# A new order for the first pair of the last stage, with two expansions inside the last convolution, and earlier middle rows behind the half quads

## What is computed

```python
for t in range(3):                                    # first block, on _gn(x)
    attn = softmax(q . (x @ Wk)); pooled = attn . (x @ Wv)
    weights = softmax(masked(pooled @ Wmlp) / 1.5); wsel = top 2 of 4, rescaled
    x_mod = x * (1 + attn_map * S * softplus(alpha))
    x = sum_e wsel[e] * conv3x3(x_mod, We[e], be[e])
x = x0 + x                                            # first residual
n = _gn(x)                                            # group norm, 32 groups
r = relu(batchnorm(n @ Wr + br)); w = r @ Ws + bs     # 9 taps for each of 16 groups
xi = n @ Wi + bi
out = x + sum over 9 taps of w * shifted(xi)          # involution, second residual
```

## Time and profile before

| | |
|---|---|
| median of three runs | 655.09 us (654.85 to 655.28) |
| the profiled execution | 654.83 us, span 653.0 us |
| PE busy | 618.9 us, 95% of the span |
| DVE busy | 529.7 us, 81% |
| ACT busy | 330.7 us, 51% |
| POOL busy | 179.1 us, 27% |
| mean granted clock of PE | 0.988 |
| share of the chain that ended last | PE 68%, DVE 10% |

### The profile page before, as it was taken

The page is one execution under the profiler, slowest core; times in us unless marked ns, Lnnn a source line. Parts: engine busy times, 40 slices in busy tenths (PEclk is TensorE's granted clock), DMA queues, the critical chain, the costliest instruction groups (busy, mean ns, idle before and its releaser), DMA issues.

```text
span 653.0 us, 15558 instructions
## 1 busy us (share of the span) xinstructions
PE 618.9 (95%) x6032; PEld 257.8 (39%) x6032; DVE 529.7 (81%) x836; ACT 330.7 (51%) x455; POOL 179.1 (27%) x193
## 2 busy tenths in 40 slices
PE   6868999989999999999999999989999999999995
PEld 6533333323343433343333434323444444444442
DVE  5789874998667977895798899768888988888885
ACT  3755443422342233233314657745777887787761
POOL 2100250005500640091028003412432342244230
PEclk9989899999999999999999999998999999999998
DMA  9940030024444245325512542000122221312222
GB/s 322 221 82 2 1 79 9 1 52 119 98 100 97 74 98 124 71 74 127 134 39 67 141 117 75 1 9 10 42 51 54 60 49 42 73 41 50 47 68 65
DMA packets 67462, 48.75 MB, mean 75 GB/s; under 512 B 53602, under 2 KB 54596, under 8 KB 67396
## 3 DMA queue, kind: packets, MB, share of 16 engines
q1 hardware_dynamic: 67108, 47.60, 29.8%
q10 hardware_dynamic: 288, 0.21, 0.1%
HBM read 35.94 MB, written 9.76 MB: 70 GB/s over the span
## 4 chain that ended last, share of the span: by engine, by line
PE 68%; DVE 10%; issue 2%; ACT 0%; DVEq 0%; ACTq 0%
PE conv L829 18%; PE conv L887 12%; PE att L903 12%; PE conv L750 10%; PE att L573 4%; PE att L652 2%; PE att L664 2%; PE att L874 2%; PE conv L769 2%; DVE xpad L1391 2%; DVE x L1763 1%; PE conv L780 1%; DVE xpad L1444 1%; DVE x L1456 1%; PE att L631 1%
## 5 line engine op out<-in xcount | busy, mean ns | idle before, releaser
L1763 DVE TENSOR_TENSOR x<-conv,x 128x512 f32<-128x512 f32 x288 | 177.8, 682 | 24.9 <-PE conv L887 23.6
L829 PE MATMUL conv<-xpad,comb 64*64 64x512 f32 x1728 | 194.1, 593 | 0.1
L829 PEld LDWEIGHTS conv<-xpad,comb 64*64 64x64 f32 x1728 | 70.4, 134 | 104.8 <-issue 102.5
L887 PE MATMUL conv<-rstack,wse 98*128 98x512 f32 x288 | 95.2, 433 | 2.7 <-DVE xin L1523 0.9
L903 PE MATMUL att<-x,cmp 64*32 64x512 f32 x1280 | 80.6, 602 | 0.0
L887 PEld LDWEIGHTS conv<-rstack,wse 98*128 98x128 f32 x288 | 48.1, 188 | 72.1 <-DVE x L1763 65.4
L1024 ACT ACTIVATE comb<-experts,small 128x768 f32<-128x768 f32 (+1 forms) x33 | 28.2, 879 | 83.9 <-PE conv L750 37.6
L1391 DVE SCALAR_TENSOR_TENSOR xpad<-att,x 128x1024 f32<-128x1024 f32 x46 | 54.3, 1212 | 18.6 <-PE att L631 18.4
L1915 POOL TENSOR_TENSOR x<-x,xin 128x1024 f32<-128x1024 f32 x15 | 35.9, 2394 | 111.6 <-ACT x L1189 111.6
L1033 ACT ACTIVATE x<-conv,bias 128x512 f32<-128x512 f32 x36 | 22.7, 681 | 75.0 <-PE conv L829 56.1
L750 PE MATMUL conv<-xpad,comb 64*64 64x512 f32 x480 | 56.4, 598 | 4.3 <-DVE x L1456 4.3
(11 more groups left out here) (225 smaller groups left out, 802.1 us busy)
## 6 DMA issues: line engine op xcount, KB each, us to landing
experts<-forms SPq DMA_DIRECT2D x88, 192.0 KB, 4.0
x<-in_x SPq DMA_DIRECT2D x32, 256.0 KB, 5.3
experts<-forms SPq DMA_DIRECT2D x56, 144.0 KB, 2.9
out<-comb SPq DMA_DIRECT2D x30, 256.0 KB, 3.2
rstack<-rstack SPq DMA_DIRECT2D x16, 128.0 KB, 2.3
experts<-in_We SPq DMA_DIRECT2D x1, 1152.0 KB
forms<-experts SPq DMA_DIRECT2D x2, 576.0 KB, 5.7
out<-comb SPq DMA_DIRECT2D x4, 128.0 KB, 2.2
```

Source lines behind the costliest of these rows:

```text
L829: last = nc.tensor.matmul(conv[own[to], h, HW * rows:HW * rows + HW], comb[own[rows], q % 2, n, tap(t)], xpad[own[rows], 2 * (q % 2) + n, ...
L887: nc.tensor.matmul(conv[:, unit, cols], wse[:, ORDER[i], :], rstk[s][0:RR, cols], start=True, stop=True).then_inc(exp_full, 1)
L1763: v.tensor_tensor(img(prod[i])[:, rows, :], img(conv[:, unit, :])[:, rows, :], xip[s][:, kh + 16 * h:kh + 16 * h + 16, kw:kw + W], ALU.mul ...
```

## The change

1. **Behind the half quads.** `hurried` leaves out quads 11 and 15, so ACT makes both of their first scaled weights and DVE's L1507 falls away there. In quads 10 and 14 `ahead` is (0,), so `middle_rows` comes behind one `modulate` instruction instead of two.
2. **Two expansions inside the last convolution.** In half 1 of quad 23, `project_xi` of pair 0 moves from behind tap 2 to behind tap 1; the expansion of index 0 stands behind tap 4 and that of index 2 behind tap 6, both in unit 0. DVE makes their products before `final(23, 1)`.
3. **Order of pair 0.** Expansions and products come in the order 0, 2, 4, 1, 6, 3, 8, 5, 7. An expansion waits for the product of index i - 2. `project` of pair 1 stands ahead of index 4, `project_xi` between 3 and 8, and the three rounds of `add_up` at the end.
4. **Statistics of quad 23** are taken by ACT (`late_stats`, with `fin` as scratch) between `empty_r` and `empty_xi` of pair 1, not by DVE between the products.
5. **Around it.** On DVE the wait for `nmr_ready` 5 stands ahead of `add_residual(22)`, and the instruction that completes `wse` moves behind it. POOL makes scale and shift (`inverse_root(4)`) after the first of two pairs of memsets. ACT waits for the pads ahead of `empty_xi` and no longer ahead of the first normalisation.

```diff
-            return q - 1 in SHORT and q % QP == QP - 1 and q < QP * LAST
+            return q - 1 in SHORT and q % QP == QP - 1 and q < QP * LAST and q - 2 not in HALF
...
-                    elif at == (3, 1, 2):
+                    elif at == (3, 1, 1):
                         project_xi(0, 0, 1)
+                    elif at == (3, 1, 4):
+                        eng.wait_ge(wse_ready, 1)
+                        eng.wait_ge(final_emptied, FINAL_PARTS - 2)
+                        expand(0, 0, AHEAD[0])
+                    elif at == (3, 1, 6):
+                        expand(0, 0, AHEAD[1])
...
+            def involve_first():
+
+                project(1, 1, 2)
+                expand(0, 0, 4)
+                eng.wait_ge(final_emptied, FINAL_PARTS)
+                expand(0, 0, 1)
+                expand(0, 0, 6)
+                expand(0, 0, 3)
+                project_xi(1, 1, 3)
+                expand(0, 0, 8)
+                expand(0, 0, 5)
+                add_up(0, 0)
+                expand(0, 0, 7)
+                add_up(0, 1)
+                add_up(0, 2)
...
                     empty_r(k + 1, 1 - s, m)
+                    if first:
+                        for n in range(2):
+                            late_stats(QUADS - 1, n, GP + QP + n, fin)
                     empty_xi(1 - s, m + 1)
...
-                            ahead = (0,) if j == 0 or q == QUADS - 2 else (0, 1)
+                            ahead = (0,) if j == 0 or q == QUADS - 2 or q - 1 in HALF else (0, 1)
...
-            final(QUADS - 1, 1)
-            eng.wait_ge(final_emptied, FINAL_PARTS)
-
...
             def involve(k, s, first=False):
-                for i in range(TAPS):
+                for i in (FIRST_ORDER[2:] if first else range(TAPS)):
                     product(k, s, i, first)
-                    if first and i in (1, 3):
-                        channel_stats(slot(QUADS - 1, i // 2))
-
+
+            for i in AHEAD[:2]:
+                product(0, 0, i, True)
+            final(QUADS - 1, 1)
+            eng.wait_ge(final_emptied, FINAL_PARTS)
```

More of the change, by code:

```diff
@@ L133, with turn_of, upto_round @@
 PARTS_OF_SUM = 4
+AHEAD = (0, 2)
+FIRST_ORDER = (0, 2, 4, 1, 6, 3, 8, 5, 7)
+def turn_of(k, i):
+    return FIRST_ORDER.index(i) if isinstance(k, int) and k == 0 else k * TAPS + i
+def upto_round(k, r):
+    if isinstance(k, int) and k == 0:
+        return max(FIRST_ORDER.index(i) for i in ROUNDS[r]) + 1
+    return k * TAPS + ROUNDS[r][-1] + 1
 def build(nc, A, out):
@@ L667, in project_xi, with expand @@
                 last.then_inc(misc_full, 1)
+            def expand(k, s, i):
+                e = turn_of(k, i)
+                unit = (s * TAPS + i) % 2
+                if i == 0:
+                    eng.wait_ge(rstk_ready, k + 1)
+                    eng.wait_ge(rhi_copied[s], 8 * (k - s) + 16)
+                for h, cols in halves():
+                    if isinstance(k, int) and k == 0 and i > 1:
+                        eng.wait_ge(prod_ready, 2 * turn_of(k, i - 2) + h + 1)
+                    elif isinstance(k, int) and k == 1 and i == 0:
+                        eng.wait_ge(prod_ready, 2 * turn_of(0, TAPS - 2) + h + 1)
+                    elif not (isinstance(k, int) and k == 0):
+                        eng.wait_ge(prod_ready, 2 * (e - 2) + h + 1)
+                    nc.tensor.matmul(conv[:, unit, cols], wse[:, ORDER[i], :], rstk[s][0:RR, cols],
+                                     start=True, stop=True).then_inc(exp_full, 1)
             def beside(p, j, h, t):
@@ L875, in turn_back @@
                 last.then_inc(misc_full, 1)
[L877 to L888, removed]
             def add_up(k, r):
@@ L905, in add_up, with involve @@
                 last.then_inc(sum_done, 1)
[L907 to L908 removed]
+            def involve_first():
[12 more added lines that the diff above has]
+                add_up(0, 2)
+            def involve(k, s, last=False):
+                m = 3 * k + 2
                 expand(k, s, 0)
[L910 to L911 removed]
                 expand(k, s, 1)
[L913 to L915 removed]
+                add_up(k - 1, 3)
+                add_up(k - 1, 4)
                 expand(k, s, 2)
@@ L929, in involve @@
                 expand(k, s, 8)
-                if not first:
-                    turn_back(k - 1, m if last else m + 2)
-            eng.wait_ge(wse_ready, 1)
+                turn_back(k - 1, m if last else m + 2)
             eng.wait_ge(late_setup, LATE_STEPS)
-            involve(0, 0, first=True)
+            involve_first()
             eng.wait_ge(misc_free, 4)
-            eng.wait_ge(late_mv_ready, GP + QP)
-            eng.wait_ge(mv_ready, NP + QP)
+            eng.wait_ge(late_mv_ready, GP + QP + 2)
+            eng.wait_ge(mv_ready, NP + 2)
             nc.tensor.matmul(att[:, 1, 0:2 * GP], pair_avg[:, :], mv[:, GP:NP, :], start=True, stop=True)\
@@ L1061, in round_attention, with late_stats @@
                 nc.scalar.activation(parts[:, :], attn[:, :], ACT.Copy).then_inc(parts_ready if n == 2 else rounded, 1)
-            def late_stats(q, n):
-                k, before = slot(q, n), 2 * (q - QP * LAST) + n
+            def late_stats(q, n, before, scratch):
+                k = slot(q, n)
                 if q in SHORT:
@@ L1212, in _ @@
             empty_r(0, 0, 0)
+            eng.wait_ge(pads_zeroed, 4)
             empty_xi(0, 1)
```

27 lines of the change are left out of this document (14 added, 13 removed).

## The result

| | before | after |
|---|---|---|
| median | 654.99 us (4 runs) | 650.1 us (4 runs: 650.0, 650.01, 650.18, 651.36) |
| ratio of the times | | 0.9929, 95% interval 0.9912 to 0.9946 |
| profiled execution, span | 654.83, 653.0 us | 651.36, 649.6 us |
| PE, DVE, ACT busy | 618.9, 529.7, 330.7 us | 618.4, 526.3, 337.1 us |

The change makes the kernel 4.9 us faster; 650.2 was forecast. The profiled execution of after is the slowest of its four, and why is told under the clock.

The account below looks back on a forecast made before the run. PE was taken as the bound nearly everywhere, so only its waits could pay. Half quads 1.2 us plus last stage 3.7 us make 4.9, taken from the median of 655.09: 650.2 us, range 648.2 to 652.6.

Parts of the forecast that it names:

- The wait for the middle rows goes: Quads 10 and 14: PE's wait for `middle_rows` disappears, gaining 1.5 us at each place.
- The map gives part of it back: Attention maps of quads 11 and 15: PE waits for `parts`, leaving 0.8 and 0.4 us of the gains.
- The term of 1.2 us: Half quads: total gain kept after the attention maps' waits, 1.2 us, with ends 0 and 3.0.
- The price of the expansions in the convolution: Quad 23's convolution: two expansions inside it push its end and the last residual later by 1.15 us.
- ACT sets the start of pair 1: Last stage: ACT's `empty_xi` ends at 447.4, after DVE; pair 1's products start at 448.9, 3.7 us sooner.
- The wait at pair 1's third expansion: Pair 1, last stage: PE's wait for DVE at the third expansion goes, gaining 0.6 us.
- The small moves: POOL's earlier scale and shift and DVE's moved wait ahead of `add_residual(22)`: costed at nothing.
- It cost little, since DVE was the slower one: Kernel before, 443.5 to 444: PE's granted clock of 0.50 was said to have cost little.
- The term of 3.7: Last stage: gain from the new order of pair 0 and the third expansion's vanished wait, 3.7 us in all.
- The sum: Whole kernel: 1.2 + 3.7 = 4.9 us off the median of 655.09, giving 650.2 us; chance 0.55.
- The clock: Rebuilt stretch of the last stage: PE is denser, so the full clock is expected instead of 0.50.
- the rival of a fall there: Last sums of pair 0 and first work of pair 1: clock falls, 1.6 us back, 651.8; chance 0.13.

Follow-up runs that it names:

- experiment 2: Kernel before with only middle rows behind one modulation in quads 10 and 14; DVE keeps its scaling in quads 11 and 15: 653.16 us, 0.9969.
- experiment 1: Kernel before with only both scalings of quads 11 and 15 on ACT and middle rows behind one modulation in quads 10 and 14: 653.02 us, 0.9975.
- experiment 4: Kernel before with the half-quad part of the change, and gathers of quads 12 and 16 not reading the routing (other outputs): 651.14 us, 0.9943.
- experiment 8: The whole changed kernel as it is, run again for comparison against the kernel before: 650.04 us, 0.9929.

## Why the prediction came out right, step by step

- **The wait for the middle rows goes: right.** 1.5 us were forecast for each. PE's way from the third row product to quad 11's first product is 238.15 - 231.20 = 6.95 us before, and 236.93 - 231.54 = 5.39 after, so 1.56 (the idle time of the earlier trace rows leaves out the tail of the product before it). The estimate of the path (one modulation and the scaling less) was right; experiment 2 shows that the modulation alone would have been enough.
- **The map gives part of it back: right in its mechanism, too large in size.** I took 0.7 and 1.1 us; the waits were 0.58 and 0.69 (with the tail of the product before them), and the gains kept are 0.97 and 0.86 and not 0.8 and 0.4. `parts` were counted on to stand still; in the trace of after the second DMA landed 0.3 and 0.5 us sooner in the frame of the quad than in that of before. Why is not shown. The term of 1.2 us measured 1.83 in this trace, 1.51 in that of experiment 1, and no less than that in any of the seven traces with this part and the old gathers (1.51 to 1.88). Its upper end, 3.0, is what experiment 4 reaches (3.1).
- **The price of the expansions in the convolution: too small.** I took 1.15 us, the pace of expansions that follow each other. The last residual starts 434.65 - 421.07 = 13.58 us after `project` of pair 0, and 434.68 - 422.75 = 11.93 before, so 1.65. The trace shows where: an expansion takes 0.67 us until the convolution goes on (429.43 to 430.10), and each of the pieces of taps around it is 0.15 us longer than its records (16 records took 1.87 us from start to start; in before 40 of them took 4.45 and 48 took 5.31, so 16 more cost 1.72).
- **ACT sets the start of pair 1: right.** 447.4 was forecast for the end of `empty_xi` with the residual at 435.8, that is 11.6 us behind it; measured 446.08 - 434.65 = 11.43. Pair 1's first product came 13.17 us behind the residual, forecast 13.1. That DVE would stand idle ahead of the second group norm for 1.5 to 2 us came out as 1.88.
- **The wait at pair 1's third expansion: half of it stayed.** 1.51 us for the four products against 1.83 before and 1.20 in pair 2; 0.3 gained where I took 0.6.
- **The small moves: not quite nothing.** POOL's scale now runs ahead of the second pair of memsets and ACT normalises at 417.45, so `project` of pair 0 comes right behind the taps: 421.07 - 414.96 = 6.11 us after their start against 422.75 - 416.46 = 6.29. 0.18 us.
- **"It cost little, since DVE was the slower one": wrong.** That was said of the fall of the clock in before. PE at half speed made DVE wait 0.67 us at 447.11 in the same trace, and the old order without this late fall is 0.77 us shorter. The term of 3.7 was added up from times that hold this cost, so it was in the sum, but under another name.
- **The sum.** 3.7 became 3.24, and 1.2 became 1.83; the two errors cancel, and that the time came out at 650.1 is in part luck. Against an old order that met the fall of the clock early, the 3.24 would be some 2.5.
- **The clock.** In the rebuilt stretch it stays at 1.00, as forecast, and so it does from 418 to 452 us in all seven profiles with the new last stage: the rival of a fall there did not come true. The row of before is in the earlier trace rows; the changed kernel, over the same place (stretch, length, busy PE, PEld, DVE, ACT, POOL, granted clock, DMA share, GB/s):

```profile
440.00:443.00 3.00, 2.73 (x29) 1.00 (x21) 3.00 (x6) 2.94 (x6) 0.83 (x1) 1.00 0.02 5
443.00:446.00 3.00, 2.73 (x34) 0.71 (x34) 1.68 (x3) 2.93 (x6) 0.00 (x0) 1.00 0.02 5
446.00:449.00 3.00, 2.87 (x38) 1.38 (x38) 2.02 (x7) 1.32 (x2) 1.32 (x1) 1.00 0.00 0
```

In the profiled execution of after it fell in the last pair instead, where it was 1.00 from 630 to 640 us in a second profile of the same kernel (that of experiment 8). Here is the first profile, and in it the sums that took 1.96 us for 16 records, against 1.09 elsewhere:

```profile
630.00:635.00 5.00, 4.70 (x23) 1.81 (x23) 3.99 (x8) 0.80 (x2) 2.37 (x1) 0.66 0.07 15
```

```profile
631.89 1.96 PE L926 MATMUL att<-x,cmp 64*32 64x512 f32 x16
```

This fits the 1.3 us that this execution took more than its three others. The rule of the Trainium skill that the prediction cited ("TensorE: Matmul & The Clock Gate", section "What's actually happening": the clock follows how busy the engine has been) is in accord with the stretch. It does not say where the fall comes: in the last pair PE waits for DVE's products in both profiles of the same program, and in only one of them did the clock fall; and before and experiment 1 have the same last stage, with the same wait of 0.87 us at its start, and the clock fell in different places.

## What to carry to other kernels

A wait that is removed is worth what the next fixed event leaves of it: look ahead on the same engine for the next thing that comes from a DMA or another engine's own chain, and subtract. To fill an idle time of one engine is worth nothing if the filling lengthens the path of the engine that starts the longest chain; compare where all the chains end, not where one is idle. A forecast that agrees in its sum should still be read term by term. And when an experiment changes one stage, measure the stages that it leaves alone too: here one of them gave 0.77 of the 1.95 us.

## What I had not expected of the hardware

An expansion (98x128 weights) put between taps of the convolution (64x64 weights, four products side by side) costs 0.82 us and not the 0.57 of one that follows another: 1.65 us for two. The trace shows the loss on both sides of the switch, about 0.1 us at the expansion and 0.15 at the taps. What makes it was not tried. And halving the gather's register loads brought its first DMAs 2.4 us forward but its last landing only 0.7 us. Last, half a clock costs by its place. In the old last stage 6.5 us of it while DVE was the slower partner (experiment 1) gave the same 32.0 us as 3 us of it there (experiment 4, at a mean of 0.58 from 436.5 to 439.5); 3 us of it where PE had to catch up cost 0.77 us more (before).
